# Rounded rows first, then remainders, in each split tile of a graph layer with residual and layer norm (one core)

## What is computed

```python
mask = adj > 0
head = mask / max(sqrt(sum(mask * mask, axis=-1)), 1e-12)
inc = adj + head
edge = (inc @ x) / sum(inc, axis=-1)
out = layernorm(x + edge, axis=-1)        # eps 1e-5
```

## Time and profile before

| | |
|---|---|
| median of 3 executions | 430.42 us (429.62 to 434.88) |
| profiled execution | 431.71 us |
| its span, first to last instruction | 429.9 us |
| mean granted TensorE clock | 0.988 |
| busy share PE / PEld | 92% / 80% |
| busy share DVE / ACT / POOL | 86% / 81% / 82% |
| HBM | 185 GB/s over the span |

### The profile page before, as it was taken

One profiled execution on the slowest core, in us unless ns is written; L12 is line 12 of the kernel. 1 busy time (PEld: TensorE's weight loads), 2 busy tenths in 40 slices (PEclk: granted clock), 3 DMA queues, 4 the chain that ended last, 5 costly groups with the idle time before them and its releaser, 6 DMA issues.

```text
span 429.9 us, 8836 instructions
## 1 busy us (share of the span) xinstructions
PE 396.9 (92%) x2152; PEld 344.8 (80%) x2152; DVE 371.7 (86%) x739; ACT 346.5 (81%) x450; POOL 351.1 (82%) x266
## 2 busy tenths in 40 slices
PE   1199767999999999999999999999999999999995
PEld 0177646888888888888888888888888888888884
DVE  0859489899999999999999999999999999999932
ACT  5766799888899889898889988888988999896200
POOL 3108069899999999999999999999999999999850
PEclk9999888999999999999999999999999999999999
DMA  8999857666656666766666666676666666660010
GB/s 233 270 240 263 242 147 220 199 189 194 197 186 199 187 202 207 220 199 192 196 187 196 191 194 197 205 219 202 192 195 194 189 196 189 196 205 24 26 38 12
DMA packets 38219, 79.85 MB, mean 186 GB/s; under 512 B 9536, under 2 KB 21824, under 8 KB 38208
## 3 DMA queue, kind: packets, MB, share of 16 engines
q1 hardware_dynamic: 37824, 78.68, 62.4%
q10 hardware_dynamic: 384, 1.05, 0.8%
HBM read 75.50 MB, written 4.19 MB: 185 GB/s over the span
## 4 chain that ended last, share of the span: by engine, by line
PE 84%; SPq 5%; issue 4%; POOL 2%; DMA 2%; DVE 1%; POOLq 0%
PE edge L618 41%; PE edge L577 21%; PE edge L621 21%; SPq L187 3%; SPq L157 2%; DMA x_stage<-in_x_dram 2%; POOL inc_split L344 2%; PE sums L572 1%; SPq L182 0%; POOL inc_split L349 0%; DVE incT L436 0%; POOL rstd L328 0%; POOLq L45 0%; DVE rows L463 0%; DVE rows L467 0%
## 5 line engine op out<-in xcount | busy, mean ns | idle before, releaser
L618 PE MATMUL edge<-x_split,inc_split 128*128 128x512 f32 (+1 forms) x810 | 281.4, 396 | 0.1
L344 POOL TENSOR_TENSOR inc_split<-incT,inc_split 128x832 fp32r<-128x832 f32 x120 | 237.2, 1987 | 10.5 <-DVE incT L436 7.6
L621 PE MATMUL edge<-x_split,inc_split 128*128 128x256 f32 x780 | 218.3, 280 | 0.0
L618 PEld LDWEIGHTS edge<-x_split,inc_split 128*128 128x128 f32 x810 | 152.9, 189 | 34.9 <-POOL inc_split L344 0.6
L220 ACT ACTIVATE sign_out<-raw,sign_bias 128x1024 bf16<-128x1024 f32 x128 | 146.4, 1144 | 32.4 <-DMA raw<-in_adj_dram 30.9
L420 DVE SCALAR_TENSOR_TENSOR inc<-raw,scaled 128x1024 f32<-128x1024 f32 x128 | 153.5, 1199 | 5.4 <-ACT scaled L231 5.4
L436 DVE STREAM_TRANSPOSE incT<-inc 128x1024 f32<-128x1024 f32 x128 | 155.4, 1225 | 0.2
L231 ACT ACTIVATE scaled<-raw,norm 128x1024 f32<-128x1024 f32 x128 | 141.7, 1108 | 13.1 <-DVE inc L420 6.6
L621 PEld LDWEIGHTS edge<-x_split,inc_split 128*128 128x128 f32 x780 | 147.7, 189 | 0.0
L577 PE MATMUL edge<-x_native,incT 128*128 128x256 f32 x384 | 96.6, 390 | 7.3 <-DVE incT L436 7.3
L577 PEld LDWEIGHTS edge<-x_native,incT 128*128 128x128 f32 x384 | 69.0, 192 | 16.4 <-DVE incT L436 8.1
(11 more groups left out here) (36 smaller groups left out, 104.9 us busy)
## 6 DMA issues: line engine op xcount, KB each, us to landing
raw<-in_adj_dram SPq DMA_DIRECT2D x504, 128.0 KB, 2.6
rows<-in_x_dram SPq DMA_DIRECT2D x32, 128.0 KB, 2.1
out_dram<-rows SPq DMA_DIRECT2D x32, 128.0 KB, 1.7
x_stage<-in_x_dram SPq DMA_DIRECT2D x8, 224.0 KB, 9.5
x_stage<-in_x_dram SPq DMA_DIRECT2D x8, 192.0 KB, 9.7
raw<-in_adj_dram ACTq DMA_DIRECT2D x8, 128.0 KB, 5.4
x_native<-in_x_dram SPq DMA_DIRECT2D x4, 192.0 KB, 7.3
```

What stands on the lines that cost most here:

```text
L344: nc.gpsimd.tensor_tensor(lo_of(s, q), incT[:, s, 0:SPLIT, q, :], hi_of(s, q).bitcast(fp32), ALU.subtract).then_inc(lo_by_pool, 1)
L618: nc.tensor.matmul(edge[s][:, c0:c1], inc_split[s][:, 0, b, :, :].rearrange("p q j -> p (q j)"), x_split[:, b, :, :].rearrange("p h d -> p ...
L621: last = nc.tensor.matmul(edge[s][:, D:2 * D], inc_split[s][:, 1, b, :, :].rearrange("p q j -> p (q j)"), x_split[:, b, 0, :], start=False ...
```

## The change

In `split_products` the loop over the blocks is cut in two: first all matmuls of rounded rows, then all matmuls of remainders. The sum is the same; the number and the shapes of the matmuls and loads are the same. Ahead of the first loop TensorE waits for the rounded quarters (two semaphores, ACT's and POOL's) instead of for the remainders; ahead of the second loop it waits for the remainders. The last matmul of the first loop signals a new semaphore, `hi_used`. ACT's `round_quarter` waits for `hi_used` of the tile two before instead of `edge_ready`, except in tile 3 (`staged`), which has no split tile before it in its slot and waits for `edge_ready` as it did. POOL's `low_quarter` and VectorE's waits are not changed.

```diff
--- before.py
+++ after.py
@@ -118,6 +118,7 @@
         hi_by_pool = sem("hi_by_pool")
         lo_by_pool = sem("lo_by_pool")
         native_done = sem("native_done")
+        hi_used = sem("hi_used")
         edge_ready = sem("edge_ready")
         dve_step = sem("dve_step")
         y_ready = sem("y_ready")
@@ -231,11 +232,12 @@
                 nc.scalar.mul(scaled[q % 2][:, :], raw[:, s, q, :], norm[:, s, q:q + 1]).then_inc(scaled_ready, 1)
 
             def round_quarter(t, s, q, reuse=True, staged=False):
-                if reuse:
+                if reuse and not staged:
+
+                    act.wait_ge(hi_used, t - 1 - FIRST_SPLIT)
+                if staged:
 
                     act.wait_ge(edge_ready, t - 1)
-                if staged:
-
                     act.wait_ge(x_lo_by_pool, len(X_LO_POOL))
                     act.wait_ge(x_lo_by_dve, len(X_LO_DVE))
                 act.wait_ge(incT_ready, G * t + q + 1)
@@ -607,7 +609,9 @@
 
             def split_products(t, s, first):
 
-                pe.wait_ge(lo_by_pool, G * (t - FIRST_SPLIT) + G)
+                t_split = t - FIRST_SPLIT
+                pe.wait_ge(hi_by_act, len(ACT_HI) * (t_split + 1))
+                pe.wait_ge(hi_by_pool, len(POOL_HI) * (t_split + 1))
                 if first:
 
                     pe.wait_ge(x_lo_by_pool, len(X_LO_POOL))
@@ -615,9 +619,13 @@
                 for b in range(SPLIT):
 
                     for c0, c1 in ((0, D), (D, 2 * D)) if b == 0 else ((0, 2 * D),):
-                        nc.tensor.matmul(edge[s][:, c0:c1], inc_split[s][:, 0, b, :, :].rearrange("p q j -> p (q j)"),
-                                         x_split[:, b, :, :].rearrange("p h d -> p (h d)")[:, c0:c1],
-                                         start=False, stop=False)
+                        last = nc.tensor.matmul(edge[s][:, c0:c1], inc_split[s][:, 0, b, :, :].rearrange("p q j -> p (q j)"),
+                                                x_split[:, b, :, :].rearrange("p h d -> p (h d)")[:, c0:c1],
+                                                start=False, stop=False)
+                last.then_inc(hi_used, 1)
+
+                pe.wait_ge(lo_by_pool, G * t_split + G)
+                for b in range(SPLIT):
                     last = nc.tensor.matmul(edge[s][:, D:2 * D], inc_split[s][:, 1, b, :, :].rearrange("p q j -> p (q j)"),
                                             x_split[:, b, 0, :], start=False, stop=(b == SPLIT - 1))
                 last.then_inc(edge_ready, 1)
```

## The result

| | before | after |
|---|---|---|
| median | 432.49 us (428.37 to 435.45, 20 runs) | 429.74 us (427.44 to 433.17, 20 runs) |
| profiled execution | 431.71 us | 431.78 us |
| its span | 429.9 us | 430.0 us |
| mean granted TensorE clock | 0.988 | 0.979 |

The ratio of after to before is 0.9948 (95% interval 0.9924 to 0.9973). The two profiled executions are equally long, so the gain cannot be read from their spans. It has to be read from the middle, and the difference at the start set against it.

What follows compares the result with a forecast made beforehand. TensorE, full in the middle, was taken as the bound. 0 us for the matmul order, -0.1 us for the waits and 0 us for the early slot gave 431.6, or 430.3 us on the median's scale; range 423 to 439.

Steps and rivals of the forecast that it cites:

- What bounds the kernel: Middle tiles: TensorE is busy 50.00 of 50.00 us without slack, so only the rate of its matmuls can move the time.
- Part 1, the term of 750 pairs: Split matmuls, regrouped: a full rounded matmul plus a remainder still takes 0.235 + 0.117 us; 750 pairs, 0 us, bounds ±7.5.
- Part 1, the reason: Split matmul steps: the excess, about a tenth, goes with the columns as a streaming rate, not a price of changing over.
- Rival (a), the alternation costs: Split matmuls: a uniform stream runs at the native step, 0.326 us a pair, POOL then binds; -14.5 us, 416 us; chance 0.08.
- Rival (b), the remainder stream outruns its loads: Steps between remainders: each costs 0.19 us for 0.117 if its load must end first; +55 us, 485 us; chance 0.09.
- Part 2, the waits: TensorE's waits for rounded rows and remainders: both met early at no cost, except -0.1 us in the first split tile.
- (c): TensorE's stream breaks at the new wait, exposing one load of 0.11 to 0.19 us a tile; 435 us; chance 0.06.
- Part 3, the early slot: ACT's rounding waits for an event 3.0 us earlier, but in the middle ACT is not free before; 0 us.

Runs made afterwards that it cites:

- e5: Kernel after with every rounded matmul of 512 columns cut into two of 256, each with its own load; ratio 1.0177 to the kernel before.
- e6: Kernel after with remainder matmuls of 128 columns instead of 256, leaving out part of the correction; one run, 423.69 us.
- e11: Kernel after with 5 native blocks instead of 6 and ACT waiting for the whole tile again; ratio 0.989 to the kernel before.
- e12: Kernel before with 5 native blocks instead of 6 and the changed matmul order alone, waits as before; ratio 1.0038 to the kernel before.
- e1: Kernel before with only the order of the matmuls changed, TensorE's and ACT's waits as before; ratio 0.9926 to the kernel before.
- e9: Kernel before, run again unchanged to see which tiles are long; one run, 431.67 us.
- e10: Kernel before, run unchanged once more for the same question; one run, 431.54 us.

## Why the prediction came out

The time, 429.74 us, is 0.1% from the 430.3 forecast. Part of that nearness is luck: the 20 executions of before have their median at 432.49 us, 0.5% above the 430.42 of 3 executions on whose scale I forecast, and the change took 0.5% off. A change of 0.5% is inside what I called the same and inside my bounds. By its steps:

- **What bounds the kernel.** Right: TensorE fills the middle of both kernels, so only its own distances could move the time.
- **Part 1, the term of 750 pairs.** Mis-sized: I put it at 0 us, from a mean of 0.350 a pair. It measured 0.347, and 750 times 0.003 are the 2.3 us found. I had worked out both lengths of a pair, 0.353 and 0.346, and averaged them without asking why there were two. The grouped order has the shorter length in every tile.
- **Part 1, the reason.** Wrong, though it gave nearly the right sum. "An excess that goes with the columns is a rate of the streaming" fails in e5: it is 0.0133 us for each split matmul. I had inferred a rate from 0.235 and 0.117, both a tenth above the array's time; but 0.235 was a step out of the alternating patterns and not the full matmul's own 0.227. A fixed sum for each matmul predicts the same total here, because their number is the same, and that is why the wrong reason was not punished. It would have been in e5, by 10 us.
- **Rival (a), the alternation costs.** It held only for the longer of the two patterns. The full step went from 0.235 to 0.227, the remainder step from 0.117 to 0.120, and against the tiles of 0.346 a pair nothing was won. The native step of 0.216 is not reached. The Trainium skill (TensorE: Matmul & The Clock Gate, "Back-to-back issue gap") gives an isolated gap of 216 ns at 512 columns. The trace has 227 in a stream of split matmuls with a load each, and the measurement decides.
- **Rival (b), the remainder stream outruns its loads.** Not reached, but near: 0.120 against the 0.11 at which the loads follow each other in e6. The row of 0.19 for a load is no price; loads follow each other at 0.11. In e6 a load and a matmul pass in 0.11 us. From the 62 ns per MATMUL that the same page of the Trainium skill ("Wait — 56ns, not 53.3ns?") states for hardware decode off, I had estimated 124 ns a remainder step, taking as much for a load; the trace, with 120 and with 110 in e6, does not agree with that estimate.
- **Part 2, the waits.** Right at this size: the first split tile's load does not wait any more, the two middle tiles shown above have no break at the second wait, each tile from 3 on takes 11.84, and (c) did not come. Whether the 0.1 us of the first split tile came cannot be read, as the clock there differed between the two executions. The price of 0 held because of the cover named for it, 0.6 us ahead of POOL; e11 and e12 show what the split wait is worth without that cover, 1.5%.
- **Part 3, the early slot.** Right. e1 has the whole gain without it at 6 native blocks, e11 at 5. In the kernel after, ACT is still in its sign pass when TensorE ends the whole tile:

ACT in order of time, kernel after, around its rounding (compare):

```profile
211.67 0.19 ACT L221 ACTIVATION_READ_ACCUMULATOR sign_out<-raw,sign_bias 128x1 f32 x1
211.76 0.87 ACT L244 CAST inc_split<-incT 128x832 fp32r<-128x832 f32 x1
```

TensorE in order of time, the end of the same tile:

```profile
208.35 3.28 PE L629 MATMUL edge<-x_split,inc_split 128*128 128x256 f32 x26
211.46 0.81 PE L579 MATMUL edge<-x_native,incT 128*128 128x256 f32 x3
```

The last remainder matmul ends at 208.35 + 3.28 = 211.63 (an end that is modelled), ACT's sign pass at 211.67 + 0.19 = 211.86, and rounding begins beside its last row at 211.76: it would have been free to start under the old wait too.

## What to carry to other kernels

On an engine that is full, count the distance from start to start for each kind of step, and where the same work takes two lengths in turn, find out why before averaging them: the shorter one may be had throughout. Split a wait for the whole of an input into waits for its parts even where it buys nothing by itself, and then move work until it does: here it let one more block go the cheap way, some 0.8% on top of the order's 0.5% (0.9871 against 0.9948, the first from four executions). And when a swap seems to convict a place, run the unchanged program twice more first.

## What the hardware showed that I had not expected

- At full clock a split matmul's step in a run of equal steps is its columns at 2.4 GHz plus 0.0133 us, 0.120 for 256 columns and 0.227 for 512 (after, e5); native matmuls go at 0.216, though at the lower clock they and the full split matmul both take 0.43 (the 10.3 us stretch of after). At the lower clock the excess is gone: 0.43 and 0.21 against 0.427 and 0.213 at 1.2 GHz.
- Alternating 512 and 256 columns goes in one of two patterns within a tile, 0.353 or 0.346 us a pair, and tiles take turns between them; which comes first differs between executions of the same program (e9, e10). The shorter one is as long as a pair in grouped order, 0.347, though neither of its steps is 0.227.
- Loads of 128 columns, each with a matmul of 128, follow each other every 0.11 us (e6), 26 in a row.
